# Later keys are set to zero by GpSimd behind the exponential, instead of masked by products ahead of it; loads are spread over attention and some work is put elsewhere

## The reference

```
x = x + 0.5 * ffn(layernorm(x))        # gate, top 2 of 8 experts, relu(x W_e + b_e), mean of the two
x = x + attn(layernorm(x))
x = x + 0.5 * ffn(layernorm(x))

attn: qkv = clip(x Wqkv^T, -8, 8); q, k = layer_norm over all 512; 32 heads of 16
      scores = q k^T / 4 + slope[h] * (key - query); later keys (key > query) masked to -1e30
      out = softmax(scores) v; out Wout^T
```

## Time and profile before

| | |
|---|---|
| median of three runs | 1007.8 us |
| profiled execution, time and span | 1013.01 us, 1011.3 us |
| PE, DVE, ACT, POOL busy | 85%, 63%, 45%, 35% of the span |
| attention, first to last key unit | 443.2 to 740.4 us |
| mean granted clock of TensorE | 0.93 of full speed |

### The profile page before, as it was taken

One profiled execution on the slowest core, in us unless ns is written; L12 is line 12 of the kernel. 1 busy time (PEld: TensorE's weight loads), 2 busy tenths in 40 slices (PEclk: granted clock), 3 DMA queues, 4 the chain that ended last, 5 costly groups with the idle time before them and its releaser, 6 DMA issues. The chain is left out here.

```text
span 1011.3 us, 19976 instructions
## 1 busy us (share of the span) xinstructions
PE 860.0 (85%) x6562; PEld 605.0 (60%) x6563; DVE 641.1 (63%) x1289; ACT 450.0 (45%) x834; POOL 353.2 (35%) x339
## 2 busy tenths in 40 slices
PE   3667999982999988879999999599988883799995
PEld 1245888862777776655555555255555552688874
DVE  7966444435888877757777777377547686444442
ACT  3531333322344433547677777367743340233331
POOL 7722777652122312210000000000234430477764
PEclk9886999995999999969999999799999996799998
DMA  9973778762355697657666666955158632478774
GB/s 345 375 283 99 130 147 152 129 112 70 91 176 184 162 228 207 200 155 147 133 128 149 138 136 138 253 130 119 35 166 286 246 115 104 97 145 152 147 134 66
DMA packets 112602, 162.06 MB, mean 160 GB/s; under 512 B 16608, under 2 KB 74080, under 8 KB 112256
## 3 DMA queue, kind: packets, MB, share of 16 engines
q1 hardware_dynamic: 94672, 123.84, 43.5%
q0 software_dynamic: 17856, 37.25, 19.9%
HBM read 97.43 MB, written 67.37 MB: 163 GB/s over the span
## 5 line engine op out<-in xcount | busy, mean ns | idle before, releaser
L870 DVE TENSOR_REDUCE att_part<-att_s_ps 128x2 f32<-128x1024 f32 (+2 forms) x160 | 195.7, 1225 | 71.0 <-PE att_s_ps L701 70.9
L827 ACT ACTIVATE att_prob<-att_st_ps 128x512 f32<-128x512 f32 x320 | 173.7, 595 | 93.8 <-PE att_st_ps L727 93.8
L146 PE MATMUL exp_z_ps<-ex_w_hi,exp_xT_hi 128*128 x312 | 131.1, 420 | 1.5 <-issue 1.2
L148 PE MATMUL exp_z_ps<-ex_w_hi,exp_xT_lo 128*128 x312 | 124.0, 398 | 0.0
L147 PE MATMUL exp_z_ps<-ex_w_lo,exp_xT_hi 128*128 x312 | 123.8, 397 | 0.0
L1632 ACT ACTIVATE exp_y<-exp_y 128x512 f32<-128x512 f32 x72 | 45.5, 632 | 166.9 <-DVE exp_y L1651 166.9
L1639 DVE TENSOR_TENSOR exp_xT_lo<-exp_t_ps,exp_xT_hi 128x512 fp32r<-128x512 f32 x78 | 54.0, 692 | 99.1 <-ACT exp_xT_hi L1623 99.1
L1218 POOL TENSOR_TENSOR ex_w_lo<-ex_w_lo,ex_w_hi 128x1024 fp32r<-128x1024 f32 x32 | 76.5, 2401 | 92.8 <-ACT ex_w_hi L1357 58.7
L740 PE MATMUL att_pv_ps<-att_prob,att_v_sb 128*32 128x256 f32 (+2 forms) x1280 | 102.2, 394 | 1.4 <-ACT wt_w_turned L832 1.4
L664 POOL CAST att_m_parts<-att_part 128x28 fp32r<-128x28 f32 x32 | 6.6, 207 | 277.1 <-DVE att_part L874 277.1
L146 PE MATMUL qkv_o_ps<-qkv_w_hi,qkv_xT_hi 128*128 128x512 f32 x192 | 81.8, 426 | 1.6 <-DVE qkv_xT_lo L455 1.6
(11 more groups left out here) (208 smaller groups left out, 1652.7 us busy)
## 6 DMA issues: line engine op xcount, KB each, us to landing
ex_w_lo<-in_L_ffn_W_e SPq DMA_DIRECT2D x32, 512.0 KB, 7.6
v_vals<-st_vals SPq DMA_DIRECT2D x16, 512.0 KB, 2.8
q_parts<-st_partq SPq DMA_DIRECT2D x32, 256.0 KB, 3.2
k_parts<-st_partk SPq DMA_DIRECT2D x32, 256.0 KB, 3.9
att_v_sb<-v_vals SPq DMA_DIRECT2D x32, 256.0 KB, 3.8
ex_bias<-in_L_attn_hidden_states SPq DMA_DIRECT2D x8, 512.0 KB, 7.7
acc<-ex_bias SPq DMA_DIRECT2D x8, 512.0 KB, 9.0
xn<-ex_rows SPq DMA_DIRECT2D x8, 512.0 KB, 5.5
```

The lines of the kernel that those rows point to most:

```text
L146: nc.tensor.matmul(out, x_hi[:, s], w_hi(c), start=(c == 0), stop=False)
L148: last = nc.tensor.matmul(out, x_lo[:, s], w_hi(c), start=False, stop=(c == C - 1))
L827: nc.scalar.activation(prob[n % 2][:, col:col + 512], st_ps[(e + half) % 3][:, :], ACT.Exp).then_inc(exp_done, 1)
L870: nc.vector.tensor_reduce(out, src, X_AXIS, ALU.max, negate=True).then_inc(red_done, 1)
```

## The change

Six things are changed. (1) The key pass has no mask products. POOL sets the exponentials of later keys in the diagonal blocks to zero by `affine_select` (`keep_earlier`), and `values` waits for POOL's `kept` where it waited for ACT's `exp_done`. The ten spare rows of each half (54 to 63) hold a coarse mask in the q and k stacks: minus 1e30 where the key's part of 47 positions lies behind the query's. (2) The query pass keeps its masks. (3) The fixed rows grow from 6 to 16 in DRAM, `load_fixed` issues six transfers for four, and their copy of 2 MB (768 KB before) stands at the start of `exp1`. (4) The nine loads of `sync_begin` and its gate stand one by one behind groups 16 to 24. (5) Wout is loaded in the q, k, v stage into a tile that is free by then; POOL splits two maxima ahead of the constants, and Wout's low part in four pieces behind groups 24 to 27. (6) In `route2` the gate of pair u - 2 stands behind the first projection of pair u, ACT copies its logits ahead of the second split, and SP loads attention output ahead of weights.

```diff
-FULL_ROWS = SCORE_ROWS + MAX_ROWS
+LATER_ROWS = HALF_ROWS - SCORE_ROWS - MAX_ROWS
+FULL_ROWS = HALF_ROWS
+FIXED_ROWS = BIAS_ROWS + MAX_ROWS + LATER_ROWS
...
+            sp.dma_start(self.q[g][base + SCORE_ROWS + MAX_ROWS:base + FULL_ROWS, :, :].bitcast(F32),
+                         self.bias_dram[0, BIAS_ROWS + MAX_ROWS:FIXED_ROWS, heads, :]).then_inc(self.loaded[g], 16)
...
-            sp.dma_start(bias_dram, bias_const).then_inc(bias_copied, 16)
...
+            sp.wait_ge(w_lo_done, 3)
+            sp.dma_start(wo_stage, w_out.rearrange("(c p) d -> p c d", p=P)).then_inc(st.wo_loaded, 16)
...
-                if n == NG - 3 * AHEAD:
-                    route.sync_begin(sp)
+                if NG // 2 <= n < NG // 2 + EARLY_LOADS:
+                    route.sync_early(sp, n - NG // 2)
...
+            def keep_earlier(n, u):
+                pool.wait_ge(exp_done, 2 * (T_UNITS * n + u) + 2)
+                at, count, step = key_blocks(u)[1]
...
+                for block in blocks:
+                    last = nc.gpsimd.affine_select(out=block, in_=block, compare_op=ALU.is_ge, fill=0.0, base=0,
+                                                   pattern=[[0, block.shape[1]], [1, P]], channel_multiplier=-1)
+                last.then_inc(kept, 1)
+            split_max(0)
+            split_max(1)
+            route.gpsimd_begin(pool)
+            for n in range(NG):
+                for u in range(T_UNITS - 1):
+                    keep_earlier(n, u)
+                if n + 2 < NG:
+                    split_max(n + 2)
+                keep_earlier(n, T_UNITS - 1)
+                if NG - 2 * C <= n < NG - C:
+                    route.gpsimd_split(pool, n - NG + 2 * C)
...
-                mask_unit(banks, where, 1)
...
-                pe.wait_ge(exp_done, 2 * T_UNITS * n + exps)
+                pe.wait_ge(kept, T_UNITS * n + units)
...
+    def sync_early(sp, step):
+        if step < EARLY_PIECES:
+            load_weights(step)
+        elif step == EARLY_PIECES:
             load_o(0)
             load_o(1)
+        elif step == EARLY_PIECES + 1:
+            load_x(0)
+            load_gate()
+        else:
+            load_x(1)
...
-            if u >= 2:
-                gate(u - 2)
...
+                    if t % 2 == 0 and u >= 2:
+                        gate(u - 2)
...
+            if u >= 2:
+                logits_out(u - 2)
             if proj and u + 1 < PAIRS:
                 o_split(2 * u + 3)
-            if u >= 2:
-                logits_out(u - 2)
...
+                sp.dma_start(copy[0], copy[1]).then_inc(copied, 16)
+                sp.wait_ge(copied, 16)
```

100 lines of the change are left out of this document (57 added, 43 removed).

## The result

The changed kernel takes 984.4 us (median of four runs, 982.3 to 987.1), the kernel before 1008.4 (four runs, 1005.7 to 1010.4): a ratio of 0.9766, with a 95% interval of 0.9732 to 0.9800. That is 24 us faster. The forecast was 979 us, with a range of 966 to 993. A run over 1.5% above the fastest of its kernel is left out of the ratios: one, of the kernel with the key masks back.

A forecast was written before the change was run, and what follows sets the result against it. Each stage has its own limit; PE bounds attention, its longest wait 11.62 us for the maximum's rows. Terms -13.5 - 13.9 + 2 - 2.5 - 7.5 + 3 + 4 = -28.4 us, from 1007.8 to 979 us; range 966 to 993.

The forecast's parts named there:

- The key masks: Attention's key pass: dropping PE's mask products gains 13.5 us, upper end 17.8, with a group at about 8.48 us.
- I take 13.5, near the start-to-start figures, since they are what PE's order sees: Attention: mask gain sized from first mask product to first score product, 13.0 us, not from mask records, 17.8.
- What hides the selects: Attention: POOL's selects, 0.41 us per 256 columns, have 2 us of cover ahead of the split; DVE's maxima stay untouched.
- The loads spread: Attention: PE's 11.62 us hole and 2.26 us at lower clock go, 13.9 us gained, with 2 us of waits left.
- so the share becomes 0.83: Attention from group 16: a 512 KB load per group lifts the DMA share from 0.57 to 0.83.
- the loads only move the stall: Attention from group 16: the maximum's rows land over 1.1 us late, losing 11.9 us; 991 us, up to 1000; chance 0.20.
- if waits for the maximum's rows add up to over 6 us: Attention: one of the signs that would show the forecast wrong, PE's waits for these rows totalling over 6 us.
- Attention's start: First groups of attention: POOL's split ahead of its constants takes 2.5 us off PE's 3.48 us wait.
- route2: Second routing stage: PE's waits of 1.12 and 0.52 us a pair go; 7.5 us gained, between 3 and 9.9.
- exp1: First expert stage: the 2 MB copy delays the second gather, costing 3 us, between 0 and 8.5.
- q, k, v: Projection stage: extra fixed-row transfers and 160 KB a group delay x for four tiles, costing 4 us, between 2.7 and 4.8.
- The early load of Wout lies in a stretch with DMA to spare: Projection stage: loading Wout there was taken to be free, with no cost in the sum.

The follow-up runs named there:

- the kernel with the burst back: The changed kernel with the nine early loads in one piece behind group 20 again; 985.1 us, 0.9726 of the kernel before.
- the better version: The changed kernel with fixed rows of q in one transfer, 2 MB copy and Wout later, expert weights in halves, values ahead of `turn_max`; 958.4 us, 0.944 of the kernel before.

## Why the prediction was right, and where it was not

The direction and the range were right. Taken between the two profiled executions the sum was -28.4 against -29.3 us measured. That is closer than its terms were, and partly luck: the masks gave 6 us more than their term and `route2` 4.3 more, the loads 6.4 less, and 5.8 us of loss had no term. Against the second profile of the changed kernel the difference is -34.6.

**The key masks** (-13.5): mis-sized. The steady group fell by 0.63 us and not by 0.39 to 0.42, 19.5 us over 31 groups. The new wait came as said (0.39 forecast, 0.43 measured), so by the waits 0.28 us a group went into it and the products were worth 0.91, where the sum had 0.63. The step that failed is "I take 13.5, near the start-to-start figures, since they are what PE's order sees". The time from the first mask product to the first score product leaves out the 0.08 to 0.09 us by which the score products behind it take longer to the next row. Units 2, 3 and 4 gave 0.65 us, where the sum had 0.39 and its upper end 0.535. The run with the masks back shows 8.90 us again. In attention as a whole the net is 10.9 to 18.8 us over five profiles, 15 on average, nearer to 13.5 than to 19.5; how much of the difference is waits brought by the shorter group is not shown.

**What hides the selects**: right in each part, 0.41 us a select, done 1.9 us ahead of the combine, maxima unchanged; the run with twice the selects shows how far off that bound was.

**The loads spread** (-13.9 + 2): the step that failed, and the reason why attention gained 19.7 and not 25.4. The figure in "so the share becomes 0.83" was worked out with the stage's mean rate, 0.26 more for 512 KB; measured was 0.31 more in the first such stretch and 0.43 in the second, over 1 in all. The 0.4 us that the masks were to take out of the slack of 1.1 were 0.63. The share and not SP's place made the rows late: 5.9 us to landing, against the 2.3 of the earlier trace rows. The rival "the loads only move the stall" was the truer description of this part, by the time of the kernel with the burst back all of it; its 991 us didn't come since the masks and `route2` gave more. The sign of being wrong, "if waits for the maximum's rows add up to over 6 us", came true: 2.24 + 0.99 + 3.28 + 1.67 + 0.68 and four smaller ones, 10.7 us in all, and the lower granted clock behind them.

**Not in the sum**: SP as the bound of the first groups. The two more transfers were priced in the q, k, v stage only, and the same `load_fixed` stands in groups 0 to 3. It cost 5.8 us in the first profile and 1.9 to 3.9 in six others. With one transfer in place of two it was 1.4 and 1.0, so a small part is not the two issues'.

**Attention's start** (-2.5): right; the wait fell by 2.3 us, the stage by 3.0.

**route2** (-7.5): the mechanism right, the size too small. Both waits went and a pair fell from 11.40 to 9.69 us. With the first pair's two waits (0.81 and 0.69), and the 1.7 us of the one pair at a granted clock of 0.87, which nothing in the sum stood for, the stage gave 11.8. The discount from 9.9 to 7.5, for limits that "no row prices", was for nothing. The old order alone gives it all back, the pair at the lower clock too.

**exp1** (+3): +2.0 in this profile, +4.0 on average of eight, inside the 0 to 8.5 given. The Trainium skill ("DMA: Bandwidth & Descriptors", "Queues, rings and completion order") has the engines take whole packets in turn, by which the cost would have lain towards 8.5 and not at the 3 taken. The runs side with neither end: in one execution the gather is 0.4 us late, in the next 7.

**q, k, v** (+4): +4.1, right by accident. The fixed rows cost 1.2 us (1.6 on average), not 4; on SP their two more issues are 0.8 us a tile (1.6 before, 2.4 after), not 1.2. "The early load of Wout lies in a stretch with DMA to spare" was the failing step: there is room on average, but 1 MB in one piece holds up the x behind it for 2.4 us, 2.9 in the end.

**From the profile to the median**: the forecast took the 5.2 us by which the profiled execution lies over the median as the same before and after. The changed kernel's profiled execution (983.8) lies at its median, so the medians differ by 23.9 us where the profiles differ by 29.2. That accounts for the 5.4 us by which 979 was too low. A second profile of the kernel before was 4.6 over again; why is open, and it may be chance.

## What to carry to other kernels

What a shorter loop gains has to be checked against everything that is paced by it: at 8.27 us a group the queue that issues was slower than the loop for four groups, and one tiny transfer often came late where a load of 512 KB stood ahead of it. Price a load by the room that is left in the one interval it falls into, ahead of the transfer that somebody waits for, and not by the stretch's mean share; and count the issues of a queue wherever the function that makes them is called. Where single executions differ by several us in one stage, compare stages over several profiles. When a term comes out right, look at its parts: the q, k, v term was right in its sum with both parts wrong, and the better version (some 3% under the changed kernel by the ratios, 5.6% under the one before) came in good part from just those.

## What the runs showed of the hardware

Not expected: what two transfers of 4 and of 10 rows cost for each half, against one of 16 with 8 KB more. Beside them four tiles of the q, k, v stage take 49.5 to 50.9 us, with the single one 45.6 to 46.7 (four kernels), and the DMA queues move more in the same time. The changed kernel:

```profile
350.00:370.00 20.00, 17.48 (x84) 13.52 (x82) 13.81 (x37) 9.16 (x21) 5.15 (x4) 1.00 0.97 224
370.00:390.00 20.00, 17.86 (x80) 14.30 (x81) 14.39 (x39) 7.62 (x17) 2.82 (x2) 0.91 0.95 244
```

The kernel with one transfer, in the same stretches:

```profile
350.00:370.00 20.00, 16.98 (x83) 13.32 (x83) 14.69 (x36) 7.84 (x18) 3.85 (x3) 1.00 1.05 270
370.00:390.00 20.00, 17.58 (x88) 13.89 (x87) 14.02 (x45) 7.82 (x18) 5.12 (x4) 1.00 1.01 260
```

224 and 244 GB/s at a share of 0.96, 270 and 260 at 1.03; the stage starts 4 us earlier in the second, so the stretches don't hold quite the same work. From 345 to 415 us the loads of x beside the stacks land 4.0 us after their issue, in the median, where they took 5.7. The issues saved on SP explain 0.2 us of a tile's 1.2. For the rest, the Trainium skill ("DMA: Bandwidth & Descriptors", "Why a DMA increments its semaphore by 16 and not by 1") states that a transfer issued from SP is split over as many engines as the largest number up to 16 that divides the outer dimension of both its sides. By it 4 rows go to four engines, 10 to ten and 16 to sixteen. The times agree in direction, but the share is a mean over all engines and no row here shows one engine, so this is a reading and not shown.

Also not expected: how far one kernel's executions differ through its transfers alone. PE's wait for the gather beside the copy was 0.4 to 7.4 us, and the loss at the spread loads 2.4 to 11.0 us, in kernels that are the same there. One profile of such a stage is one throw; the size of a wait for a transfer in a full queue needs several.
